# The experts phase of a transformer kernel: GpSimd weighs VectorE's product before the down projection, and all 18 down products of a group add up in one PSUM bank

## The reference

```python
combine = (jax.nn.one_hot(topk_idx, E, dtype=tw.dtype) * tw[..., None]).sum(1)
h = jnp.einsum('td,edf->etf', x, gate_w)
u = jnp.einsum('td,edf->etf', x, up_w)
y = jnp.einsum('etf,efd->etd', jax.nn.silu(h) * u, down_w)
routed = jnp.einsum('etd,te->td', y, combine)
sh = jax.nn.silu(x @ sh_gate_w) * (x @ sh_up_w) @ sh_down_w
return (routed + sh).reshape(hidden_states.shape)
```

## Time and profile before

| | value |
|---|---|
| median of the runs | 2280.21 us |
| the profiled execution, its own time | 2276.67 us |
| its span in the trace | 2274.7 us |
| PE busy | 2021.8 us, 89% |
| DVE busy | 1738.6 us, 76% |
| ACT busy | 1015.3 us, 45% |
| POOL busy | 511.8 us, 23% |
| mean granted TensorE clock | 0.95 of full speed |
| DMA moved | 30.41 MB, 13 GB/s |

### The profile page before, as it was taken

The page is one execution under the profiler, slowest core; times in us unless marked ns, Lnnn a source line. Parts: engine busy times, 40 slices in busy tenths (PEclk is TensorE's granted clock), DMA queues, the critical chain, the costliest instruction groups (busy, mean ns, idle before and its releaser), DMA issues. The chain is left out here.

```text
span 2274.7 us, 52942 instructions
## 1 busy us (share of the span) xinstructions
PE 2021.8 (89%) x19268; PEld 1557.3 (68%) x19268; DVE 1738.6 (76%) x4586; ACT 1015.3 (45%) x1956; POOL 511.8 (23%) x504
## 2 busy tenths in 40 slices
PE   5999995777777999997999997994999999999998
PEld 3666664566664666664677675764888888888887
DVE  4767766677755888887799995665888888888886
ACT  3455452445542444443455553543444444443443
POOL 0101100000001222322122222663222232232221
PEclk9999998899996999998999998996999999999999
DMA  3000000000000000000000001000000000000000
GB/s 121 20 28 28 18 18 1 1 1 0 0 1 1 1 0 0 0 0 19 30 28 28 28 18 63 1 0 0 6 6 10 5 5 10 5 5 9 6 5 10
DMA packets 27248, 30.41 MB, mean 13 GB/s; under 512 B 1936, under 2 KB 20624, under 8 KB 26896
## 3 DMA queue, kind: packets, MB, share of 16 engines
q1 hardware_dynamic: 27152, 29.28, 4.1%
HBM read 25.08 MB, written 4.19 MB: 13 GB/s over the span
## 5 line engine op out<-in xcount | busy, mean ns | idle before, releaser
L320 ACT ACTIVATE ex<-ps 128x512 f32<-128x512 f32 x384 | 228.7, 596 | 335.7 <-PE ps L580 334.5
L1102 ACT ACTIVATE moe_sg<-ps 128x512 f32<-128x512 f32 x288 | 172.6, 599 | 365.0 <-PE ps L1154 364.8
L414 DVE TENSOR_REDUCE mx<-ps 128x8 f32<-128x512 f32 x384 | 262.5, 684 | 62.0 <-PE ps L562 61.2
L580 PEld LDWEIGHTS ps<-pack,sh 128*128 128x128 f32 x1536 | 173.9, 144 | 185.0 <-DVE sh L416 113.3
L580 PE MATMUL ps<-pack,sh 128*128 128x128 f32 x1536 | 253.7, 289 | 44.4 <-DVE sh L416 43.1
L1138 PEld LDWEIGHTS ps<-down,moe_act 128*128 128x128 f32 x2048 | 266.1, 191 | 33.9 <-DVE moe_acc L1331 13.0
L1138 PE MATMUL ps<-down,moe_act 128*128 128x128 f32 x2048 | 271.0, 275 | 7.3 <-DVE moe_acc L1331 7.3
L416 DVE TENSOR_TENSOR sh<-ps,mx 128x512 f32<-128x512 f32 x384 | 265.6, 692 | 13.2
L596 PEld LDWEIGHTS ps<-vblk,ex 128*64 128x64 f32 x6144 | 215.1, 140 | 66.8 <-issue 66.2
L596 PE MATMUL ps<-vblk,ex 128*64 128x32 f32 x6144 | 258.1, 228 | 0.3
L1313 DVE TENSOR_TENSOR moe_act<-ps,moe_sg 128x512 f32<-128x512 f32 x288 | 197.7, 686 | 69.2 <-PE ps L1154 55.2
(11 more groups left out here) (232 smaller groups left out, 3663.7 us busy)
## 6 DMA issues: line engine op xcount, KB each, us to landing
ctxT<-in_ctx SPq DMA_DIRECT2D x32, 256.0 KB, 2.8
x_res<-in_x SPq DMA_DIRECT2D x16, 256.0 KB, 2.9
kmi<-in_key_mask SPq DMA_DIRECT2D x16, 256.0 KB, 3.4
out<-moe_acc SPq DMA_DIRECT2D x16, 256.0 KB, 2.3
pack<-in_pack SPq DMA_DIRECT2D x1, 2536.5 KB, 9.2
wqkv<-in_wqkv SPq DMA_DIRECT2D x1, 1536.0 KB, 8.5
gate<-in_gate SPq DMA_DIRECT2D x6, 192.0 KB, 4.0
up<-in_up SPq DMA_DIRECT2D x6, 192.0 KB, 4.1
```

The source lines that it names most:

```text
L320: nc.scalar.activation(ex[:, u % 2], UB[u % 4].rearrange("p (c n) -> p c n", n=P), ACT.Exp).then_inc(e_ready, 1)
L414: nc.vector.tensor_reduce(mx[:, u % 2], sc, AX.X, ALU.max).then_inc(max_done, 1)
L580: last = nc.tensor.transpose(UB[u % 4][:, c * P:(c + 1) * P], sh[:, u % 4, c * P:(c + 1) * P], ident)
L1102: nc.scalar.activation(sg[:, k % 2], GB_[k % 2], ACT.Silu).then_inc(silu_done, 1)
```

## The change

The down projection is turned round. The down weights are now the stationary operand and the activation of all 512 tokens is the moving one, so an expert costs one product of 128x512 in float32, its output has features on partitions, and all 18 of a group accumulate in one PSUM bank. A weight per token is then a weight per column, which has to be applied before the product: GpSimd's new `weigh` multiplies `moe_act` with the expert's weight row, which must stand on all 128 partitions (`wide_w`, in the memory of `y_res`), into `moe_wact`. The rows come there by way of a transpose of `moe_comb` on PE (`turn_weights`), a copy on ACT (`copy_combT`), four DMAs to DRAM and 16 broadcast DMAs back, 256 KB each (`spread_weights` on SP). At the end of a group the sum is copied (`copy_yT`), turned back by four transposes (`turn_sum`) and added to the residual once (`add_up`); the accumulations on DVE, ACT and GpSimd are gone. The gate bank now waits for `silu_done` instead of `act_ready`, DVE's product waits for `weighed` of expert k-3, and some routing parts stand behind other experts.

```diff
+            def spread_weights(g, more):
+                sp.wait_ge(combT_copied, nth(g))
...
+                for t in range(TILES):
+                    sp.dma_start(comb_dram[:, t * P:(t + 1) * P], combT[t * E:(t + 1) * E, :]).then_inc(comb_kept, 16)
+                sp.wait_ge(comb_kept, nth(g) * 16 * TILES)
+                sp.sem_inc(passed, 1)
+                for e in range(E):
+                    if more:
+                        sp.wait_ge(weighed, (g - 1) * E + (e + 1))
+                    sp.dma_start(wide_w[:, e, :], comb_dram[e:e + 1, :].partition_broadcast(P)
+                                 ).then_inc(wide_loaded[e], 16)
...
-            def add_part(g, j):
-                if j > 1:
-                    pool.wait_ge(part_added, nth(g, len(OTHERS) - 1, j - 2))
-                pool.wait_ge(acc_done, nth(g, K - 1, OTHERS[j] - SH + 1))
-                nc.gpsimd.tensor_tensor(part[:, 0], part[:, 0], part[:, j], ALU.add).then_inc(part_added, 1)
...
+            def weigh(g, e):
+                k = e + SH
+                pool.wait_ge(wide_loaded[e], nth(g) * 16)
+                pool.wait_ge(act_ready, nth(g, K, k))
+                nc.gpsimd.tensor_tensor(wact[:, e % 3], act_[:, k % 3], wide_w[:, e, :], ALU.mult).then_inc(weighed, 1)
...
             def step(g, s, first, more):
+                for k in range(K):
+                    if k >= SH:
+                        weigh(g, k - SH)
+                    if more and k == 1:
+                        scale_rows(g + 1)
+                    if more and k == 4:
+                        low_rows(g + 1, 1 - s)
+                    if more and k == 11:
+                        rank_experts(g + 1)
...
+            def turn_weights(g):
+                pe.wait_ge(routing, nth(g, NR, NR - 1))
+                nc.tensor.transpose(CB, comb[:, :, :].rearrange("p a e -> p (a e)"), C["ident"]).then_inc(combT_ready, 1)
...
+            def down_proj(g, s, k, first):
+                if k < SH:
+                    pe.wait_ge(act_ready, nth(g, K, k))
+                else:
+                    pe.wait_ge(weighed, nth(g, E, k - SH))
...
+                last = nc.tensor.matmul(YB[s], down[:, k, :], act_[:, k] if k < SH else wact[:, (k - SH) % 3], start=k == 0, stop=k == K - 1)
...
+            def turn_sum(g):
+                pe.wait_ge(yT_copied, nth(g))
+                for t in range(TILES):
+                    last = nc.tensor.transpose(XB[:, t * P:(t + 1) * P], yT[:, t * P:(t + 1) * P], C["ident"])
...
                     if k >= 2:
+                        pe.wait_ge(silu_done, nth(g, K, k - 2))
+                    elif not first:
+                        pe.wait_ge(silu_done, g * K + (k - 1))
+                    product(GB_[k % 2], gate_hi[:, k], gate_lo[:, k], x_hi[:, s], x_lo[:, s]).then_inc(g_ready, 1)
...
-                    if k >= 2:
-                        down_proj(g, k - 2, first)
+                    if k >= LAG - 1:
+                        down_proj(g, s, k - (LAG - 1), first and k - (LAG - 1) == 0)
...
+                    if not first and k == TURN_Y:
+                        turn_sum(g - 1)
+                    if more and k == 15:
+                        turn_weights(g + 1)
...
                 if k >= SH + 3:
-                    dve.wait_ge(y_ready, nth(g, K - 1, k - SH - 2))
...
+                    dve.wait_ge(weighed, nth(g, E, k - 3 - SH))
...
+            def add_up(g, s):
+                dve.wait_ge(y_ready, nth(g))
+                dve.wait_ge(stored[s], g * 8 + (1 - 8 * s))
+                V.tensor_tensor(acc[:, s], XB.rearrange("p (t d) -> p t d", d=D), tiles_of(x_res, g), ALU.add
+                                ).then_inc(totals, 1)
...
-            ROUTE_SLOTS = (6, 7, 8, 9, 10, 11, 14, 16)
+            ROUTE_SLOTS = (6, 7, 8, 8, 9, 10, 13, 14)
```

More of the change, by code:

```diff
@@ L872, with experts_phase @@
 CH = 3
-def experts_phase(nc, ps, C, x_res, gate, up, down, w_loaded, out):
+def experts_phase(nc, ps, C, x_res, y_res, gate, up, down, w_loaded, comb_dram, out):
     with ExitStack() as ctx:
@@ L930, in experts_phase @@
         winv = sb("winv", [P, TILES])
-        comb = sb("comb", [P, 2, TILES, E])
+        comb = sb("comb", [P, 2, TE])
+        combT = sb("combT", [P, P])
         GB_ = [ps[:, i, :] for i in (0, 1)]
@@ L952, in experts_phase @@
         routing = sem("routing")
-        comb_ready = sem("comb_ready")
+        comb_set = sem("comb_set")
+        combT_ready = sem("combT_ready")
+        combT_copied = sem("combT_copied")
+        comb_kept = sem("comb_kept")
+        wide_loaded = [sem(f"wide_loaded{e}_") for e in range(E)]
         g_ready = sem("g_ready")
@@ L1076, in high_weights, with copy_combT, copy_yT @@
                     nc.scalar.copy(up_hi[:, part], up[:, part]).then_inc(w_high, 1)
+            def copy_combT(g, first):
+                act.wait_ge(combT_ready, nth(g))
+                if not first:
+                    act.wait_ge(comb_kept, g * 16 * TILES)
+                nc.scalar.copy(combT[:, :], CB).then_inc(combT_copied, 1)
+            def copy_yT(g, s):
+                act.wait_ge(yT_ready, nth(g))
+                nc.scalar.copy(yT[:, :], YB[s]).then_inc(yT_copied, 1)
             def prep(g, s):
@@ L1081, in prep @@
                 route_exp(g, s)
-            def weigh_expert(g, s, j, first):
-                k = OTHERS[j]
-                n = k - SH + 1
-                if j == 0:
-                    act.wait_ge(routing, nth(g, NR, NR - 1))
-                    if not first:
-                        act.wait_ge(totals, g)
-                act.wait_ge(y_ready, nth(g, K - 1, n))
-                act.wait_ge(acc_done, nth(g, K - 1, n - 1))
-                for t in range(TILES):
-                    last = nc.scalar.activation(part[:, j, t], YB[k % 2][:, t * D:(t + 1) * D], ACT.Copy,
-                                                scale=comb[:, s, t, k - SH:k - SH + 1])
-                last.then_inc(acc_done, 1)
+                copy_combT(g, True)
             def step(g, s, first, more):
@@ L1101, in step @@
                     act.wait_ge(g_ready, nth(g, K, k))
+                    if k >= 2:
+                        act.wait_ge(act_ready, nth(g, K, k - 2))
+                    elif not first:
+                        act.wait_ge(act_ready, g * K + (k - 1))
                     nc.scalar.activation(sg[:, k % 2], GB_[k % 2], ACT.Silu).then_inc(silu_done, 1)
-                    if k - 3 in OTHERS:
-                        weigh_expert(g, s, OTHERS.index(k - 3), first)
-                    if more and k == 3:
+                    if not first and k == COPY_Y:
+                        copy_yT(g - 1, 1 - s)
+                    if more and k == 4:
                         copy_xT(g + 1, 1 - s)
@@ L1175, in step @@
                         logits(g + 1, 1 - s)
+                    if not first and k == TURN_Y:
+                        turn_sum(g - 1)
+                    if more and k == 15:
+                        turn_weights(g + 1)
                 if not more:
-                    down_proj(g, K - 2, False)
-                    down_proj(g, K - 1, False)
+                    for k in range(K - (LAG - 1), K):
+                        down_proj(g, s, k, False)
+                    turn_sum(g)
             pipelined(pe, NG, prep, step)
@@ L1346, in step @@
                         norm_stats(g + 1, 1 - s)
-                    if more and k == 2:
+                    if more and k == 1:
                         norm_apply(g + 1, 1 - s)
+                    if not first and k == ADD_Y:
+                        add_up(g - 1, 1 - s)
                     for part, at in enumerate(ROUTE_SLOTS):
@@ L1352, in step @@
                 if not more:
-                    for k in range(K - 3, K):
-                        accumulate(g, s, k)
+                    add_up(g, s)
+            V.memset(comb[:, :, :], 0.0).then_inc(comb_set, 1)
+            dve.wait_ge(comb_set, 1)
             pipelined(dve, NG, prep, step)
@@ L2017, in build @@
                     for i in range(K // CH) for buffer, array in ((gate, gate_in), (up, up_in), (down, down_in))])
-        experts_phase(nc, ps, C, x_res, gate, up, down, w_loaded, out)
+        experts_phase(nc, ps, C, x_res, y_res, gate, up, down, w_loaded, comb_dram, out)
 def kernel(**inputs):
```

132 lines of the change are left out of this document (52 added, 80 removed).

## The result

The changed kernel takes 2349.79 us (median of 4 runs, 2344.94 to 2353.49) against 2281.34 for the kernel before beside it: ratio 1.0301, 95% interval 1.028 to 1.0321, slower. The forecast was 2346. The profiled execution took 2353.49 us, with a span of 2351.4.

What follows compares the result with a forecast made beforehand. PE bounds the experts phase, VectorE close behind. 15 intervals of 42.2 + 5.8 = 48.0 instead of 43.66 give +65, start +3: 2345 on the profiled execution, 2348 for a median, said as 2346; range 2292 to 2364.

Steps and rivals of the forecast that it cites:

- TensorE's own work: Experts phase: eight narrow matmuls (0.89 us an expert) become one wide product (0.86); a group needs 42.2 us, practically as before.
- VectorE's lost 13.5 us a group: Experts phase: VectorE loses the accumulations, 215.6 us in the phase, 13.5 a group; its own load is no bound any more.
- The held instructions: Routing on VectorE: small SBUF instructions wait until GpSimd's whole instruction is over, so products and weighings run late; forecast case 0.60.
- The ledger: Queues of VectorE and GpSimd followed from gate 6: product 10 at 15.35 us (due 11.0), weighing 12 done at 25.5 (wanted 19.7).
- The stalls: PE is 5.8 us late at the down product of expert 12, in two or three stalls at downs 9, 10 and 12.
- the rival that only the shown forms are held: Routing beside weighings: stall 2.4, interval 44.6 us, 2297; chance 0.20 together with the case of 1.09 us weighings.
- The start: Start of the experts phase: turn_weights puts 12 wide matmuls behind the wait for the routing, 2.8 us, taken as 3.
- The weights for turn_weights: Next group's weights, due by T16: between in time and 1.0 us late; taken as in time, lateness (2363 and up) 0.08.
- The broadcasts: 16 broadcasts of 256 KB a group, each landing in 2.9 us; about five us of slack, so no cost.
- the tail: End of the phase: accumulate and total exchanged for copy, transposes and one addition; even.

Runs made afterwards that it cites:

- narrow weighing: Changed kernel with GpSimd weighing only the first 128 of each expert's 512 token columns, the rest left out of the sum: 2265.97 us.
- halved weighing: Changed kernel with each weighing split into two GpSimd instructions of 256 columns: 2346.55 us.
- early start: Changed kernel with the first group's transposition of the weights behind the gate and up products of experts 0 and 1: 2355.76 us.
- thin rows: Changed kernel whose broadcast DMAs bring only the first 128 of the 512 columns of each weight row: 2345.52 us.
- late transposition: The unread weights kernel with the transposition of the weights moved from behind expert 15 to behind expert 17: 2326.96 us.
- paired version: Shared version with routing gathered behind products 6, 8, 10, 12, 14, 15, GpSimd also weighing 7, 9, 11, 13, plus the early start: 2286.89 us, ratio 1.0033.
- unread weights: Changed kernel whose down products read the unweighed product, six buffers deep; GpSimd still makes the weighed products, which nothing reads: 2371.84 us.
- shared version: Changed kernel with VectorE weighing experts 6 to 14 and ranking, GpSimd weighing the others, routing spread, transposition behind expert 17: 2307.91 us, ratio 1.012.

## Why the prediction was right

Step by step:

- TensorE's own work: one wide float32 product in place of eight narrow ones was put at 0.86 against 0.89, a step at 2.25. Steps without a wait are 2.24, and the narrow weighing gives 42.27 of work against the 42.2 of the sum. Right.
- VectorE's lost 13.5 us a group buy nothing. Right: 142 us less work on the page, and the time rose.
- The held instructions. The ledger put products 6 to 10 at 2.41, 4.95, 7.85, 11.6 and 15.35 behind gate 6; they start at 2.51, 4.95, 7.87, 11.52 and 15.10. Weighing 12 was put at 25.5; its down product starts at 2101.91, 24.98 behind gate 6. The forms held here are those with two inputs in SBUF; that the weighing is held in its turn behind product 10 was forecast and is there.
- The stalls: down products 9, 10 and 12 were named, and these wait. 5.8 us a group were predicted, 48.0 of interval; most groups take 47.9 to 48.1. The mean from gate 6 to gate 6 is 48.16.
- That every routing instruction with two inputs in SBUF is held goes beyond the rows of before, which have moe_gout, ff_se and moe_masked; it was the author's estimate. The changed kernel's trace shows it in the forms that meet a weighing (medians): moe_kept, moe_gsc, moe_w and moe_comb are held (1.34, 1.26, 1.24 and 1.10 us, 0.18 to 0.23 where they met none), the reciprocal isn't (0.178), nor the product, which takes one input from PSUM (0.691). In the halved weighing, whose instructions take 0.738, moe_kept takes 0.78: the hold goes by the instruction. The prediction's wider sentences, that a small VectorE instruction on SBUF waits for GpSimd and that none that reads SBUF ran freely beside it, don't hold: beside the reciprocal there is moe_rank, a reduction of one SBUF tile, which takes 1.22 us in both kernels beside a GpSimd instruction (15 of 16 groups) as without one. The number of inputs is not all of it: moe_gout has one tensor input, and in the kernel before it took 1.23 to 1.27 us in the 7 of 16 groups where a GpSimd addition ran beside it (0.17 elsewhere). In the changed kernel it never met one. By the rival that only the shown forms are held it would have been 2297.
- The start: 3 predicted, 2.1 shown by the early start, and 2.0 from the end of the first routing to gate 6 (1593.07 - 1577.3 against 1585.30 - 1571.5). The weights for turn_weights were taken as in time and are 0.34 us late.
- The broadcasts: each was taken to land like x_res, in 2.9 us, and sixteen in a row land in 6.2 at the median. The five us of slack covered it, and the thin rows show that it costs nothing. A mis-sized term, without effect.

The sum from its parts: 15 intervals from gate 6 to gate 6, +69.1 (predicted 65); the start +2.0 (predicted 3); the tail -0.2 (predicted even). Together the phase from the end of its first routing takes 774.1 us against 703.2 (2274.7 - 1571.5), +70.9 where 68 were predicted. The intervals are 4 us over the forecast, and 3.3 of them are the three groups that the slow clock made 1.1 us longer. The profiled execution's remaining 5.8 us lie ahead of the phase, in stretches that the change doesn't touch.

One step was right in its number and incomplete in its reason. The forecast followed the down product of expert 12 and took the next group's weights as just in time. The version in which nobody reads a weighed product shows that both are the same chain, GpSimd's ranking behind held work: take away the first wait, and the second stands 4.4 us behind it. And behind some of the waits the granted clock falls to 0.50, which no term of the forecast has. In the changed kernel most of that is hidden under the next wait: from gate 6 to down 12 the time is what GpSimd's ledger says, with slow matmuls or without. It shows in three groups of fifteen, where it is small against the whole; that it stayed small was not reasoned but luck. The late transposition shows the case where it does cost, 1.7 us a group.

What stays open: how the remaining 2 us of interval in the paired version divide (1.2 us a group are recorded waits), what held the one-input moe_gout before, and whether weighings shorter than 1.29 us exist on this engine for the whole 512 columns in this phase (a multiply of that shape took 1.09 in the phase before); none was tried.

## What to carry to other kernels

Before handing work to an idle GpSimd, ask what VectorE runs beside it: a GpSimd instruction of 1.3 us makes a 0.2 us VectorE instruction with two SBUF inputs last 1.3 us, so the price is at most (number of meetings) x (length of the GpSimd instruction), and it is paid on VectorE's path, not on GpSimd's. Count the meetings by writing the two queues beside each other from one product on; it came out here within 0.3 us for five products and 0.5 for weighing 12. If the work must go to GpSimd, put it where VectorE has little of that form to do. That, together with five weighings and the ranking given to VectorE, a later transposition and an early start, took back some 60 of the 68 us; which of these did how much was not measured one by one. And don't take away one wait without asking which comes next.

## What the runs showed of the hardware that was not expected

- A wait was followed by a loss beyond its length in some groups and not in others. In the late transposition, behind waits of 2.08 to 2.26 us, the granted clock was 0.57 to 0.65 over 4 us in eleven of fifteen groups (matmuls of 128x512 of 0.63 instead of 0.40 us, 1.7 us lost) and stayed at 1.00 in four. In the unread weights, with a wait of 4.4 us that ends at 2064.81, it was 1.00 up to 2063.0 and 0.50 in each half microsecond from 2063.5 to 2069.5. In the changed kernel, behind waits of 0.38 and 1.30 close together, it fell in three of the fourteen groups that have both (0.57 over 4 us in each), and behind the 2.1 us at down 12 in four of the other twelve. In the paired version, whose waits from 1584 to 2280 us are 0.5 at the longest, it was 1.00 in every stretch of 4 us there.
- The GpSimd product takes 0.462 us for 128 columns (the shorter weighing), 0.738 for 256 (the two halves) and 1.289 for 512 (the changed kernel). That is some 0.19 us and 2.15 ns a column, so the two halves together (1.48) cost 0.19 more than the whole.
- Where VectorE does all the weighings, a weighing, which needs the 128x512 product just before it, starts 0.79 us behind that product's start (2008.98 to 2009.77), where an instruction that doesn't need it starts at 0.60; it is 0.87 in the shared version (2015.74 to 2016.61), where the weighing also waits for the count of weighed products.
- In the early start gate 2 still waited 2.26 us for ScalarE. Its timeline has the copy of the weights (0.27 us, at 1581.83), an ACT_TABLE_LOAD (1.28 us, at 1582.11) and then its first Silu of the phase (at 1583.41).
